# First attention of a two-layer transformer kernel: each step reordered into four stages of two key tiles

## The chip, the cores and the metric

One core of one Trainium2 chip. The metric is the device time of one execution in microseconds (us); the whole two-layer program is one launch. Everything is fp32 at the interface. Four engines compute: TensorE (PE, with its weight loads shown as PEld), VectorE (DVE), ScalarE (ACT) and GpSimd (POOL); SyncE (SP) issues the DMAs.

## The reference

Two pre-layernorm layers over x of shape (2, 1024, 128). Only the first attention matters here:

```python
q = z @ wq @ fcq_w + fcq_b
k = z @ wk @ fck_w + fck_b
v = z @ wv @ fcv_w + fcv_b          # 16 heads of 64
scores = jnp.einsum('bihd,bjhd->bhij', q, k) / scale
attn = jax.nn.softmax(scores, axis=-1)
out = jnp.einsum('bhij,bjhd->bihd', attn, v)
return out.reshape(b, n, N_HEAD * D_V) @ fco_w + fco_b
```

After it come a mixture of experts, a second (causal) attention with rotary parts, and a second mixture of experts. None of their code changes.

## The kernel before

The first attention (`l0_attention`) runs 16 steps, two batches of 8 head pairs. Step n does the attention of its own pair, and beside it prepares step n + 1 and finishes step n - 1. The engines follow one script per step, `step_script(n)` (L391), which TensorE, ScalarE and VectorE all walk; two tables, `AFTER_SCORES` and `AFTER_VALUES` (L375 to L383), say where the small units stand in it. Its items:

- **ST(kt, j)**, the scores of key tile kt (of 8, 128 keys each) for query half j, transposed (keys on partitions), both heads: 4 matmuls of 128x512 in fp32r (L931, L932), accumulating two operand parts. The array is used whole (128x128). ScalarE takes the exponential into `prob[kt % 4]` (L680).
- **PV(kt, j)**, the values: fp32 matmuls of 64 columns by 512, the two heads side by side in the two column halves of the array (L904), accumulating over kt in `pv`. One PV is 4 matmul records (two heads, each fp32 product in two passes).
- **s(x)**, x = 0 to 15, for the next step: the scores of 128 queries against 512 keys, only to find each query's maximum; the two heads use the two row halves of the array, 64 rows each (L863, L865), and VectorE reduces the tile (L738, `mx`).
- **q(j)**: the next step's projection, 4 fp32r matmuls on the whole array (L854), rounded and copied by ScalarE (L638), the rest taken by VectorE (L732).
- **m**: VectorE takes the larger of the two key halves' maxima (`mmax`, L742), TensorE turns them (L883, 16 rows), VectorE makes a row of them (`mrow`, L747), and a DMA (L528) writes it as row 0 of `q2`, where the next step's score matmuls (L932) read it as the shift of the softmax. Before its first ST, step n waits for that row (`row_loaded`, L925).
- **l, r, n, g** for the step before: softmax sums through a matmul with ones (L888, 32 columns of the array), reciprocal, normalisation (L775), output projection in fp32 on the whole array (L893) and the addition into the output (L779). **R, X, P** are early pieces of the next layer that stand in three of the last steps.

Each ST and each unit that TensorE writes takes the next of three PSUM tiles `pair0` to `pair2` (`RING = 3`), in the order of the script; before it writes one, TensorE waits until the tile three places earlier has been read (`await_buffer`, L479). GpSimd adds the `prob` tiles up for the sums (L623, L628). In steps 0 to 11 a piece of the later layers' weights is loaded, split in two parts (ScalarE L655, VectorE L812, after the step's units) and stored.

Before the change a step is, for each key tile: two ST, then the units of `AFTER_SCORES`, then the two PV of the key tile before, then those of `AFTER_VALUES`. The PV of the last key tile stand in the next step. Runs of matmuls that use the array in one way are thus: ST ST | s s | PV PV | s | and so on.

## Time and profile before

| | us |
|---|---|
| median of 3 runs (1487.17 to 1487.96) | 1487.65 |
| the profiled execution's own time | 1486.37 |
| its span, first to last instruction | 1484.6 |
| first attention, from the first score of step 0 to the end of the last matmul for the sums | 63.84 to 747.85 |
| mean granted TensorE clock over the span | 0.972 |

How to read the profile: busy is the time in which at least one instruction of the engine runs. Matmul records overlap (one of 512 columns lasts 0.39 to 0.50 us but the next begins 0.23 us later), so TensorE's progress is read from the start of one matmul to the start of the next, not from durations. A timeline row gives start, length, engine, line, operation, tiles and count, and in brackets how long the engine sat idle before it and what ended that.

### The profile page before, as it was taken

The page shows a single profiled execution, that of the slowest core. Times are in us where ns is not written, and L with a number is a line of the kernel's source. Part 1 is how long each engine was busy: PE and PEld are TensorE (multiplying, and loading weights), DVE is VectorE, ACT ScalarE, POOL GpSimd, SP SyncE. Part 2 cuts the span into 40 slices and gives each one's busy share as a digit, 9 for nine tenths or more (in the row PEclk, how much of TensorE's full clock was granted, in tenths as well). Part 3 has the DMA queues.
Part 4 walks back from the last instruction along what each step waited for, and adds up shares of the span by engine and source line. Part 5 has one row for each costly group of instructions (what it writes and reads, how often), then busy time and mean ns, then how long its engine had stood idle before and what let it go on. Part 6 is the DMA issues. An engine that isn't in the chain of part 4 may idle for free. (4 is left out here: it accounts for less than half of the span.)

```text
span 1484.6 us, 18636 instructions
## 1 busy us (share of the span) xinstructions
PE 1381.6 (93%) x6322; PEld 783.4 (53%) x6322; DVE 999.2 (67%) x1675; ACT 817.5 (55%) x1236; POOL 863.1 (58%) x685
## 2 busy tenths in 40 slices
PE   6699999999999999999978977899999997999998
PEld 5344444444444444544456734454444445787776
DVE  5676777777677777677666678676666725566665
ACT  4244444444444445444545443566776565787776
POOL 0298777777977777787744505455565332344443
PEclk9699999999999999999999997999999998999999
DMA  3110111111011111000050005012111106000000
GB/s 107 33 44 16 58 59 44 58 58 48 26 58 58 51 52 44 15 16 15 26 159 1 1 0 100 15 24 30 21 30 29 30 2 271 1 1 8 8 8 8
DMA packets 32586, 60.59 MB, mean 41 GB/s; under 512 B 9499, under 2 KB 17084, under 8 KB 32348
## 3 DMA queue, kind: packets, MB, share of 16 engines
q1 hardware_dynamic: 32492, 59.40, 14.4%
q8 instruction: 51, 0.84, 0.2%
q14 instruction: 43, 0.35, 0.1%
HBM read 35.13 MB, written 13.89 MB: 33 GB/s over the span
## 5 line engine op out<-in xcount | busy, mean ns | idle before, releaser
L628 POOL TENSOR_TENSOR psum_k<-psum_k,prob 128x1024 f32<-128x1024 f32 x186 | 457.9, 2485 | 46.5 <-ACT prob L680 46.5
L680 ACT ACTIVATE prob<-pair 128x1024 f32<-128x1024 f32 x256 | 250.5, 1025 | 378.7 <-PE pair L932 378.7
L738 DVE TENSOR_REDUCE mx<-pair 128x2 f32<-128x1024 f32 x256 | 305.3, 1222 | 100.0 <-PE pair L865 99.5
L904 PE MATMUL pv<-prob,c_all 128*64 128x512 f32 x1024 | 247.9, 605 | 0.0
L1935 DVE CUSTOM_DVE_ANT_0 l_banks<-l_banks,causal 128x128 f32<-128x128 f32 (+7 forms) x256 | 189.5, 782 | 75.8 <-PE l_banks L1973 74.7
L931 PE MATMUL pair<-qq,ak 128*128 128x512 f32 x512 | 221.5, 433 | 7.1 <-DVE q L732 3.3
L1843 ACT ACTIVATE l_prob<-l_banks 128x1024 f32<-128x1024 f32 (+7 forms) x256 | 155.3, 654 | 111.7 <-PE l_banks L1992 111.0
L932 PE MATMUL pair<-q,kb 128*128 128x512 f32 x512 | 202.4, 395 | 0.0
L2151 POOL TENSOR_TENSOR silu_rest_t<-silu_t,silu_lead_t 128x512 fp32r<-128x512 f32 x74 | 96.4, 1304 | 145.0 <-ACT silu_lead_t L2348 145.0
L1897 POOL TENSOR_SCALAR_AFFINE_SELECT l_prob<-l_prob 128x128 f32<-128x128 f32 x256 | 72.3, 295 | 146.9 <-ACT l_prob L1843 145.3
L623 POOL TENSOR_TENSOR psum_k<-prob 128x1024 f32<-128x1024 f32 x31 | 74.1, 2412 | 118.9 <-ACT prob L680 118.9
L931 PEld LDWEIGHTS pair<-qq,ak 128*128 128x128 f32 x512 | 96.6, 189 | 73.2 <-issue 22.8
L2517 DVE TENSOR_TENSOR silu_t<-silu_t,bank_t 128x512 f32<-128x512 f32 x128 | 88.0, 688 | 64.4 <-ACT silu_t L2339 60.4
L1973 PE MATMUL l_banks<-l_kk,l_qq 128*128 128x512 f32 (+3 forms) x384 | 115.4, 394 | 14.1 <-DMA l_qq<-rounded 4.7
L2339 ACT ACTIVATE silu_t<-bank_t,b_t 128x512 f32<-128x512 f32 x144 | 99.3, 690 | 41.8 <-PE bank_t L951 41.6
L904 PEld LDWEIGHTS pv<-prob,c_all 128*64 128x64 f32 x1024 | 62.1, 136 | 112.6 <-issue 80.6
L863 PE MATMUL pair<-ak,qq 64*128 64x512 f32 x256 | 112.8, 487 | 9.0 <-DVE mx L738 5.0
L1992 PE MATMUL l_banks<-l_qq,l_kk 128*128 128x512 f32 (+3 forms) x384 | 112.1, 385 | 4.2 <-DVE plain L1935 3.2
L865 PE MATMUL pair<-kb,qq 64*128 64x512 f32 x256 | 113.1, 488 | 0.0
L863 PEld LDWEIGHTS pair<-ak,qq 64*128 64x128 f32 x256 | 47.0, 188 | 122.0 <-issue 94.6
L932 PEld LDWEIGHTS pair<-q,kb 128*128 128x128 f32 x512 | 96.9, 189 | 19.8 <-issue 3.3
L1973 PEld LDWEIGHTS l_banks<-l_kk,l_qq 128*128 128x128 f32 x384 | 64.9, 199 | 73.7 <-ACT l_prob L1843 23.6
(318 smaller groups left out, 2276.8 us busy)
## 6 DMA issues: line engine op xcount, KB each, us to landing
plain<-scratch_sums SPq DMA_DIRECT2D x32, 256.0 KB
whole<-in_experts SPq DMA_DIRECT2D x12, 512.0 KB, 5.1
scratch_lead<-rounded SPq DMA_DIRECT2D x12, 512.0 KB, 2.6
scratch_rest<-rounded SPq DMA_DIRECT2D x12, 512.0 KB, 3.9
w_lead_t<-scratch_lead SPq DMA_DIRECT2D x9, 512.0 KB, 6.6
w_rest_t<-scratch_rest SPq DMA_DIRECT2D x9, 512.0 KB, 7.4
l_kk<-rounded SPq DMA_DIRECT2D x16, 256.0 KB, 4.2
l_qq<-rounded SPq DMA_DIRECT2D x16, 256.0 KB, 5.4
```

Source lines behind the costliest of these rows:

```text
L628: nc.gpsimd.tensor_tensor(total[:, h, :], total[:, h, :], prob[kt % 4][:, h, :], ALU.add).then_inc(summed, 1)
L680: nc.scalar.activation(prob[kt % 4][:, :, ts(j, BLK)], buffer("ST", at)[:, :, :], ACT.Exp, scale=D0 ** -0.5).then_inc(exp_done, 1)
L738: nc.vector.reduce_max(mx[:, x % 2, :, x // 2], buf[:, :, :], AX.X).then_inc(read, 1)
L863: nc.tensor.matmul(buf[:, 0, :], qq[k % 2][0][0:D0, ts(t, P)], m.ak[0:D0, keys], start=True, stop=True)
L865: ins = nc.tensor.matmul(buf[:, 1, :], qq[k % 2][1][D0:P, ts(t, P)], m.kb[D0:P, keys], start=True, stop=True)
L904: ins = nc.tensor.matmul(pv[D0 * h:D0 * (h + 1), ts(j, BLK)], m.c_all[:, TT * (s // PAIRS) + kt, :], prob[kt % 4][:, h, ts(j, BLK)], start ...
L931: nc.tensor.matmul(buf, m.ak[:, keys], qq[n % 2][h][:, ts(j, BLK)], start=True, stop=False)
L932: ins = nc.tensor.matmul(buf, m.kb[:, keys], q2[n % 2][:, h, ts(j, BLK)], start=False, stop=True)
L1843: nc.scalar.activation(prob[kt % 2][:, g, P * kt:T], buffer(item)[:, P * kt - T:], ACT.Exp, scale=SCALE1).then_inc(exp_done, 1)
L1935: ins = nc.vector.tensor_tensor_reduce(scores[:, 0:s_width(t)], scores[:, 0:s_width(t)], hidden, 1.0, -3e38, ALU.add, ALU.max, mx[:, g, t: ...
L1973: ins = nc.tensor.matmul(out[:, lo:end], qq[k % 2][:, g, ts(t, P)], kk[k % 2][:, g, lo:end], start=True, stop=True)
L1992: ins = nc.tensor.matmul(buf[:, at:at + end - lo], kk[n % 2][:, g, ts(kt, P)], qq[n % 2][:, g, lo:end], start=True, stop=True)
```

## The change

The two tables give way to one, `STAGES`, that writes a step as four stages of two key tiles. Stage 0 holds four ST together, q(0), four PV (key tiles 6 and 7 of the step before) and l. Stages 1 to 3 hold four ST each, and between them all 16 s units (6, 5 and 5), then four PV of the two key tiles of the stage before. In stage 3 the PV are broken by m and g. The PV of the last two key tiles stand in the next step (of the last step: behind the loop). The larger of the two halves' maxima is no longer taken by VectorE ahead of m: TensorE turns both halves (two matmuls), and VectorE reduces over them in PSUM and then makes `mrow`. On the SP queue the row of shifts (`shift_rows`) now goes ahead of the row of maxima. ScalarE's early work of the next layer hangs on later key tiles.

```diff
--- before.py
+++ after.py
@@ -372,15 +372,17 @@
             + [("l", 0), ("r", 0), ("n", 0), ("g", 0)] * k_done)
 
 
-AFTER_SCORES = {
-    0: [("q", 0), ("q", 1)],
-    1: [("s", 1), ("s", 2)], 2: [("s", 4), ("s", 5)], 3: [("s", 7), ("s", 8)], 4: [("s", 10), ("s", 11)],
-    5: [("s", 13), ("s", 14)],
-}
-AFTER_VALUES = {
-    0: [("s", 0)], 1: [("s", 3), ("l", 0)], 2: [("s", 6), ("X", 0)], 3: [("s", 9), ("r", 0)], 4: [("s", 12)],
-    5: [("s", 15)], 6: [("m", 0), ("n", 0), ("R", 0), ("P", 0)], 7: [("g", 0)],
-}
+STAGES = [
+    ["ST", "ST", "ST", "ST", ("q", 0),
+     "PV", "PV", "PV", "PV", ("l", 0)],
+    [("s", 0), "ST", "ST", ("s", 1), "ST", ("s", 2), "ST", ("s", 3), ("q", 1), ("s", 4), ("s", 5),
+     "PV", "PV", "PV", "PV", ("X", 0), ("r", 0)],
+    [("s", 6), "ST", "ST", ("s", 7), "ST", ("s", 8), "ST", ("s", 9), ("s", 10),
+     "PV", "PV", "PV", "PV", ("n", 0)],
+    [("s", 11), "ST", ("s", 12), "ST", ("s", 13), "ST", ("s", 14), "ST", ("s", 15),
+     "PV", "PV", ("m", 0), "PV", ("g", 0), "PV", ("R", 0), ("P", 0)],
+]
+STRIDE = TT // len(STAGES)
 
 
 STATISTICS_BEHIND = (3, 8)
@@ -392,12 +394,15 @@
 
     has = step_units(n + 1 < STEPS0, n > 0) + EARLY.get(n, [])
     out = []
-    for kt in range(TT):
-        out += [("ST", kt, 0), ("ST", kt, 1)]
-        out += [("UNIT",) + u for u in AFTER_SCORES.get(kt, []) if u in has]
-        if kt or n:
-            out += [("PV", kt - 1, 0), ("PV", kt - 1, 1)]
-        out += [("UNIT",) + u for u in AFTER_VALUES.get(kt, []) if u in has]
+    for stage, items in enumerate(STAGES):
+        at = {"ST": 2 * STRIDE * stage, "PV": 2 * STRIDE * (stage - 1)}
+        for item in items:
+            if item in at:
+                if at[item] >= 0 or n:
+                    out.append((item, at[item] // 2, at[item] % 2))
+                at[item] += 1
+            elif item in has:
+                out.append(("UNIT",) + item)
     return out
 
 
@@ -463,7 +468,6 @@
         on = sb("on", [P, T])
         ones = sb("ones", [P, D0])
         mx = sb("mx", [P, 2, 2, TT])
-        mmax = sb("mmax", [P, 2, TT])
         tcol = sb("tcol", [2 * TT, P])
         mrow = sb("mrow", [2 * TT, P], F32R)
         whole = sb("whole", [P, PIECE])
@@ -487,7 +491,7 @@
         row_loaded, m.sums_moved, inv_ready = sem("row_loaded"), sem("sums_moved"), sem("inv_ready")
         sums_moved = m.sums_moved
         filled, read = sem("work_filled"), sem("work_read")
-        hi_done, mmax_ready = sem("hi_done"), sem("mmax_ready")
+        hi_done, top_ready = sem("hi_done"), sem("top_ready")
         st_filled, exp_done, pv_done, ut_ready = sem("st_filled"), sem("exp_done"), sem("pv_done"), sem("ut_ready")
         summed, norm_done = sem("summed"), sem("norm_done")
         piece_in, piece_led, piece_split, piece_kept = (sem("piece_in"), sem("piece_led"), sem("piece_split"),
@@ -586,8 +590,8 @@
                 if n:
                     sums(n - 1, place(n, ("l", 0)))
                 if n + 1 < STEPS0:
+                    shift_rows(n + 1)
                     max_rows(n + 1, place(n, ("m", 0)))
-                    shift_rows(n + 1)
             sums(LAST, first_of(STEPS0))
             sp.wait_ge(row_loaded, 32 * STEPS0)
             sp.wait_ge(cols_loaded, 16 * STEPS0)
@@ -664,7 +668,7 @@
                             project(n + 1, rest[1], place(n, tuple(rest)))
                     elif what == "PV":
                         kt, j = rest
-                        if kt < 0:
+                        if kt == -1:
                             keep_product(n - 1, j)
                     else:
                         kt, j = rest
@@ -681,30 +685,30 @@
                                              scale=D0 ** -0.5).then_inc(exp_done, 1)
                         if j and kt in (4, 5) and piece_of(n) is not None:
                             lead_piece(piece_of(n), kt - 4)
-                        if j and kt == 2 and n == AT_TURN:
+                        if j and kt == 3 and n == AT_TURN:
 
                             act.wait_ge(read, place(PAIRS, ("g", 0)) + 1)
                             act.wait_ge(piece_split, 2 * len(PIECES))
                             nc.scalar.activation(turned[:, :], m.out_t[:, 0:T], ACT.Identity, bias=m.out_bias[:, 0:1]
                                                  ).then_inc(early_act, 1)
-                        if j and kt == 6 and n == AT_ROOT:
+                        if j and kt == 7 and n == AT_ROOT:
                             act.wait_ge(m.aggr_done, NBLK + 2)
                             nc.scalar.activation(m.std0[:, 0:HALF], m.mv[:, 0:HALF, 1], ACT.Sqrt, bias=m.eps[:, 0:1]
                                                  ).then_inc(early_act, 1)
-                        if j and kt < 2 and n == AT_LOGITS:
+                        if j and kt in (1, 3) and n == AT_LOGITS:
 
                             act.wait_ge(early_dve, CENTRE)
                             act.wait_ge(read, place(AT_TURN, ("R", 0)) + 1)
-                            for t in range(TPB * kt, TPB * (kt + 1)):
+                            for t in range(TPB * (kt // 2), TPB * (kt // 2 + 1)):
                                 ins = nc.scalar.activation(normal[:, t, :], m.x[:, t, :], ACT.Identity,
                                                            bias=m.centre[:, t:t + 1], scale=m.rstd0[:, t:t + 1])
                             ins.then_inc(early_act, 1)
-                        if j and kt == 4 and n == AT_LOGITS:
+                        if j and kt == 5 and n == AT_LOGITS:
 
                             act.wait_ge(read, place(AT_LOGITS, ("X", 0)) + 1)
                             act.wait_ge(piece_kept, 32 * len(PIECES))
                             nc.scalar.copy(m.early_x[:, 0, :], xt[:, :]).then_inc(early_act, 1)
-                        if j and kt == 0 and n == LAST:
+                        if j and kt == 1 and n == LAST:
                             act.wait_ge(early_dve, SHIFTED)
                             nc.scalar.activation(m.ex[:, :, :], m.lg[:, :, :], ACT.Exp).then_inc(early_act, 1)
             for j in R2:
@@ -736,15 +740,14 @@
                 elif kind == "s":
                     v.wait_ge(filled, u + 1)
                     nc.vector.reduce_max(mx[:, x % 2, :, x // 2], buf[:, :, :], AX.X).then_inc(read, 1)
-                    if x == S_UNITS - 1:
-
-                        v.wait_ge(read, u + 1)
-                        nc.vector.tensor_tensor(mmax[:, :, :], mx[:, 0, :, :], mx[:, 1, :, :], ALU.max
-                                                ).then_inc(mmax_ready, 1)
                 elif kind == "m":
                     v.wait_ge(cols_loaded, 16 * (k + 1))
                     v.wait_ge(filled, u + 1)
-                    nc.vector.scalar_tensor_tensor(mrow[:, :], buf[0:2 * TT, 0, 0:P], -1.0, tcol[:, :],
+                    top = buf[0:2 * TT, 1, 0:P]
+                    nc.vector.reduce_max(top, buf[0:2 * TT, 0, 0:2 * P].rearrange("p (a n) -> p n a", a=2), AX.X
+                                         ).then_inc(top_ready, 1)
+                    v.wait_ge(top_ready, k + 1)
+                    nc.vector.scalar_tensor_tensor(mrow[:, :], top, -1.0, tcol[:, :],
                                                    ALU.mult, ALU.subtract).then_inc(read, 1)
                 elif kind == "l":
                     v.wait_ge(filled, u + 1)
@@ -879,9 +882,11 @@
                         ins = nc.tensor.matmul(buf[:, 0, ds(NEXP * t, NEXP)], xt[:, ts(t, P)], m.wr[:, :],
                                                start=True, stop=True)
                 elif kind == "m":
-                    pe.wait_ge(mmax_ready, k + 1)
-                    ins = nc.tensor.matmul(buf[0:2 * TT, 0, 0:P], mmax[:, :, :].rearrange("p h t -> p (h t)"),
-                                           m.ident[:, :], start=True, stop=True)
+                    pe.wait_ge(read, place(k - 1, ("s", S_UNITS - 1)) + 1)
+                    for half in R2:
+                        ins = nc.tensor.matmul(buf[0:2 * TT, 0, ts(half, P)],
+                                               mx[:, half, :, :].rearrange("p h t -> p (h t)"), m.ident[:, :],
+                                               start=True, stop=True)
                 elif kind == "l":
                     await_sums(pe, k, TT - 1)
                     for q in range(4):
@@ -932,8 +937,9 @@
                             ins = nc.tensor.matmul(buf, m.kb[:, keys], q2[n % 2][:, h, ts(j, BLK)],
                                                    start=False, stop=True)
                         ins.then_inc(st_filled, 1)
-            for j in R2:
-                product(STEPS0 - 1, TT - 1, j)
+            for kt in range(TT - STRIDE, TT):
+                for j in R2:
+                    product(LAST, kt, j)
             u = first_of(STEPS0)
             unit("l", 0, u, LAST)
```

How the order moves, at three places. Names: `pair0` to `pair2` are the ring of PSUM tiles, qq and ak, kb and q2 the operands of the scores, and the brackets name the semaphores that a row waits for (work_read: a unit's tile was read; exp_done: an exponential was taken).

TensorE, a key tile in the middle of a step, before:

```order
L931 MATMUL pair1<-qq00,ak 128x512 [waits work_read]
L932 MATMUL pair1<-q2_0,kb 128x512
L931 MATMUL pair1<-qq01,ak 128x512
L932 MATMUL pair1<-q2_0,kb 128x512
L863 MATMUL pair2<-ak,qq10 128x512 [waits work_read]
L865 MATMUL pair2<-kb,qq11 128x512
L863 MATMUL pair0<-ak,qq10 128x512 [waits hi_done,exp_done]
L865 MATMUL pair0<-kb,qq11 128x512
L904 MATMUL pv<-prob2,c_all 64x512 [waits exp_done]
L904 MATMUL pv<-prob2,c_all 64x512
L904 MATMUL pv<-prob2,c_all 64x512 [waits exp_done]
L904 MATMUL pv<-prob2,c_all 64x512
```

and with the change, a piece of stage 2:

```order
L866 MATMUL pair1<-ak,qq10 128x512 [waits work_read]
L868 MATMUL pair1<-kb,qq11 128x512
L936 MATMUL pair2<-qq00,ak 128x512 [waits exp_done]
L937 MATMUL pair2<-q2_0,kb 128x512
L936 MATMUL pair2<-qq01,ak 128x512
L937 MATMUL pair2<-q2_0,kb 128x512
L866 MATMUL pair0<-ak,qq10 128x512 [waits hi_done,exp_done]
L868 MATMUL pair0<-kb,qq11 128x512
L936 MATMUL pair1<-qq00,ak 128x512 [waits work_read]
L937 MATMUL pair1<-q2_0,kb 128x512
L936 MATMUL pair1<-qq01,ak 128x512
L937 MATMUL pair1<-q2_0,kb 128x512
```

What moved: two ST in a row (8 matmuls) and two s in a row have become one ST, one s, one ST, one s; the PV went behind the stage.

TensorE, around the maxima at the end of a step, before:

```order
L904 MATMUL pv<-prob1,c_all 64x512 [waits exp_done]
L904 MATMUL pv<-prob1,c_all 64x512
L883 MATMUL pair2<-ident,mmax 16x128 [waits mmax_ready,work_read]
L931 MATMUL pair0<-qq00,ak 128x512 [waits exp_done]
L932 MATMUL pair0<-q2_0,kb 128x512
L931 MATMUL pair0<-qq01,ak 128x512
L932 MATMUL pair0<-q2_0,kb 128x512
L931 MATMUL pair1<-qq00,ak 128x512 [waits exp_done]
```

and with the change:

```order
L909 MATMUL pv<-prob0,c_all 64x512 [waits exp_done]
L909 MATMUL pv<-prob0,c_all 64x512
L887 MATMUL pair1<-ident,mx 16x128 [waits work_read]
L887 MATMUL pair1<-ident,mx 16x128
L909 MATMUL pv<-prob1,c_all 64x512 [waits exp_done]
L909 MATMUL pv<-prob1,c_all 64x512
L898 MATMUL pair2<-on,g_all 128x512 [waits norm_done,exp_done]
L898 MATMUL pair2<-on,g_all 128x512
L909 MATMUL pv<-prob1,c_all 64x512 [waits exp_done]
L909 MATMUL pv<-prob1,c_all 64x512
```

What moved: m has two matmuls and waits for the last reduction itself; the unit g, which stood directly ahead of the next step's scores, is now between two PV.

VectorE, the same place, before:

```order
L738 TENSOR_REDUCE mx<-pair0 128x2 [waits work_filled]
L742 TENSOR_TENSOR mmax<-mx 128x16 [waits work_read]
L747 SCALAR_TENSOR_TENSOR mrow<-pair0,tcol 16x128 [waits work_filled,cols_loaded]
L775 TENSOR_TENSOR on<-plain 128x1024 [waits ut_ready,sums_moved]
L779 TENSOR_TENSOR plain<-pair0,plain 128x1024 [waits work_filled]
L812 TENSOR_TENSOR rounded<-whole,rounded 128x512 [waits piece_kept,piece_led] x2
L732 SCALAR_TENSOR_TENSOR q2_0<-pair0,q_bias,qq00 64x512 [waits hi_done]
```

and with the change:

```order
L742 TENSOR_REDUCE mx<-pair2 128x2 [waits work_filled]
L742 TENSOR_REDUCE mx<-pair1 128x2 [waits work_filled]
L747 TENSOR_REDUCE pair2<-pair2 16x128 [waits work_filled,cols_loaded]
L750 SCALAR_TENSOR_TENSOR mrow<-pair2,tcol 16x128 [waits top_ready]
L782 TENSOR_TENSOR plain<-pair0,plain 128x1024 [waits work_filled]
L815 TENSOR_TENSOR rounded<-whole,rounded 128x512 [waits piece_kept,piece_led] x2
L736 SCALAR_TENSOR_TENSOR q2_0<-pair2,q_bias,qq00 64x512 [waits hi_done]
```

What moved: `mmax` is gone, a reduction from PSUM into PSUM stands ahead of `mrow`, and the normalisation (`on`) has gone up to the end of stage 2.

## Rows read from the trace of the kernel before

**Rows 1.** The page, busy time of each engine, share of the span, instructions.
```profile
PE 1381.6 (93%) x6322; PEld 783.4 (53%) x6322; DVE 999.2 (67%) x1675; ACT 817.5 (55%) x1236; POOL 863.1 (58%) x685
```
**Rows 2.** Stretches, one per step: length; busy PE, PEld, DVE, ACT, POOL; clock; DMA.
```profile
63.84:104.56 40.72, 39.63 (x163) 20.33 (x163) 27.24 (x24) 19.11 (x22) 28.46 (x12) 0.96 0.04 14
104.56:146.51 41.95, 41.95 (x185) 20.74 (x183) 27.44 (x26) 19.88 (x24) 35.30 (x16) 1.00 0.16 52
146.51:189.54 43.03, 42.63 (x184) 20.62 (x183) 31.25 (x28) 19.96 (x24) 33.93 (x15) 1.00 0.16 50
...
620.64:663.27 42.63, 42.32 (x185) 20.64 (x183) 30.06 (x42) 21.69 (x25) 33.12 (x15) 1.00 0.06 14
663.27:710.30 47.03, 45.37 (x209) 23.27 (x207) 35.90 (x33) 23.02 (x31) 35.67 (x15) 1.00 0.07 21
710.30:747.85 37.55, 37.53 (x158) 16.80 (x156) 25.50 (x45) 18.30 (x22) 25.31 (x9) 1.00 0.06 15
```
**Rows 3.** Timeline of step 7, one key tile: PV, s, ST, s.
```profile
377.65 1.94 PE L904 MATMUL pv<-prob,c_all 128*64 128x512 f32 x8
378.13 0.14 PEld L904 LDWEIGHTS pv<-prob,c_all 128*64 128x64 f32 x2 [0.28 <-ACT prob L680]
...
378.56 0.14 PEld L904 LDWEIGHTS pv<-prob,c_all 128*64 128x64 f32 x2 [0.29 <-issue]
...
379.52 0.50 PE L863 MATMUL pair<-ak,qq 64*128 64x512 f32 x1
...
379.95 0.50 PE L931 MATMUL pair<-qq,ak 128*128 128x512 f32 x1
...
380.06 1.23 DVE L738 TENSOR_REDUCE mx<-pair 128x2 f32<-128x1024 f32 x1 [0.21 <-PE pair L865]
380.29 0.40 PE L932 MATMUL pair<-q,kb 128*128 128x512 f32 x1
...
380.52 0.40 PE L931 MATMUL pair<-qq,ak 128*128 128x512 f32 x1
...
382.01 0.50 PE L863 MATMUL pair<-ak,qq 64*128 64x512 f32 x1
```
**Rows 4.** Timeline of step 7, the unit m and what follows.
```profile
399.00 0.39 PE L883 MATMUL pair<-ident,mmax 128*16 128x128 f32 x2
...
399.32 0.50 PE L931 MATMUL pair<-qq,ak 128*128 128x512 f32 x1
```
**Rows 5.** Timeline, turn from step 6 to step 7.
```profile
360.21 1.98 PE L893 MATMUL pair<-on,g_all 128*128 128x512 f32 x4
...
361.63 0.80 PE L931 MATMUL pair<-qq,ak 128*128 128x512 f32 x1
...
362.26 0.40 PE L932 MATMUL pair<-q,kb 128*128 128x512 f32 x1
...
363.37 3.47 DVE L812 TENSOR_TENSOR rounded<-whole,rounded 128x512 fp32r<-128x512 f32 x2
...
366.87 2.77 DVE L732 SCALAR_TENSOR_TENSOR q<-pair,q_bias,qq 64x512 fp32r<-64x512 f32 x4
...
367.66 0.49 PE L863 MATMUL pair<-ak,qq 64*128 64x512 f32 x1
...
368.35 0.50 PE L931 MATMUL pair<-qq,ak 128*128 128x512 f32 x1 [0.20 <-DVE q L732]
...
370.95 0.50 PE L863 MATMUL pair<-ak,qq 64*128 64x512 f32 x1
```
**Rows 6.** ScalarE's exponentials, steps 3 to 12: duration ns min/median/max.
```profile
L680 ACT ACTIVATE prob<-pair x160: 1016/1026/1030, 191.1 to 617.5; 128x1024 f32<-128x1024 f32 x160
```
**Rows 7.** Timeline, ahead of step 0: the row of maxima and the first score.
```profile
61.90 0.60 SPq L528 DMA_DIRECT2D q<-mrow  x1
...
63.84 0.77 PE L931 MATMUL pair<-qq,ak 128*128 128x512 f32 x1 [2.37 <-issue]
```
**Rows 8.** Timeline of step 6, VectorE's maximum of two halves.
```profile
353.44 1.58 DVE L742 TENSOR_TENSOR mmax<-mx 128x16 f32<-128x16 f32 x1
```

## Prediction

> **What bounds the kernel now.** I read the page first: TensorE is busy 93% of the span, the next engine (VectorE) 67% [rows 1]. An average says little, so I cut the first attention into its steps. A typical step lasts 43.03 us, and in it TensorE is busy 42.63, GpSimd 33.9, VectorE 31.3, ScalarE 20.0, at granted clock 1.00 [rows 2]. Step 2 is shown; steps 3 to 11 last as long to 0.02 us, so what is said of one holds for all. Busy time doesn't tell whether TensorE streams or only drains, so the timeline is next, read from start to start.
>
> In one key tile [rows 3] four PV (two items, 8 records) take from 377.65 to 379.52, 1.87 us; one s unit takes 0.43 to the next ST; two ST take from 379.95 to 382.01, 2.06 us. Inside a run the pitch is 0.23 us per fp32r matmul (380.29 to 380.52) and 0.43 per fp32 pair (weight loads at 378.13 and 378.56); the two heads of an s unit run at once and count as one. So the content is 8 x 0.23 = 1.84 for the two ST, 0.23 for s, 4 x 0.43 = 1.72 for the PV, and what is over, 0.20 to 0.22, 0.20 and 0.15, comes once for each run that uses the array in one way. The first gap of a run shows half of it: 379.95 to 380.29 is 0.34, not 0.23. I call it the price of a run: **0.20 us for an fp32r run, 0.15 for a PV run.** Where the shape stays the same nothing is paid: the unit g takes 1.42 to the following ST, and that one's first gap is 0.63 where 0.34 is usual, together 1.71 us = 4 x 0.43 [rows 5].
>
> The rest are waits. Behind the turn of a step, s lasts 0.69 (367.66 to 368.35) and two ST 2.60 (to 370.95) [rows 5]: 0.26 and 0.54 over their usual, **0.80 us**. The cause stands beside: VectorE finishes the rest of the weight piece (from 363.37, 3.47 us) and only then takes q (from 366.87), so the ring tiles of q come free late. Further on in the step the key tiles repeat rows 3, with nothing waiting. TensorE's own sequence is therefore the bound, and the change has to be counted in runs.
>
> **The change, part by part**, for one step.
>
> *Runs.* Before, a step has 8 runs of ST (q and g join one), 11 of s, 8 of PV, and l and m: 29. After: whole-array runs 1 + 4 + 3 + 4 (stage 0 joins four ST and q(0); in stages 1 to 3 each s breaks the ST) and g, which now stands alone between PV: 13. Runs of s: 5 + 4 + 5 = 14. Runs of PV: one in each of stages 0 to 2, three in stage 3 (broken by m and g): 6. With l and m 35. That is 8 fp32r runs more, 8 x 0.20 = +1.60 us, and 2 PV runs fewer, -0.30 us. The price of a run of four ST is not in the trace. Bounds: 0, as where q follows ST in the same shape (a pair of runs that differ in nothing but weights), and 0.22, as for eight ST. It is nearest to the latter, since the neighbours (s on row halves) are the same; I take 0.20.
>
> By the Trainium skill (TensorEngine Tiling (Array Packing), Key Properties) a change of tiling mode drains the array; this speaks against the change, and the trace agrees on when a price is paid. For its size the skill has only a nearby figure (TensorE: Matmul & The Clock Gate, Single matmul latency: 398 cycles besides the columns, 0.166 us warm); the estimate from that page would make the 8 runs 1.33 us, and the sum of all steps 4 us lower, 1496 us.
>
> *m.* Two matmuls take the place of one. m lasted 0.32 us [rows 4]; with twice the records between 0.40 and 0.64, I take 0.56: +0.24 us. VectorE loses `mmax`, 1.58 us [rows 8], and gains a short reduction. mmax lay beside PV and cost nothing where PV follow; it costs nothing now. If it had been exposed, m would have waited: no row shows that.
>
> *The turn of the step.* Four ST, q(0), then 3.6 us of PV and 1.0 of l, before s(0) at 9.4 us. VectorE's piece ends 5.2 us into the step, half of q's 2.77 follows: 1.4 us, done by 7.8 even if ScalarE is late. The wait of 0.80 us goes, and nothing is late in its place. q(1) is covered by the PV of stage 1.
>
> *The ring.* New borders are tight. From the start of an s to that of the ST two places on is 0.43 + (0.34 + 3 x 0.23 + 0.10 = 1.13) + 0.43 = 1.99 us. In that time the tile must be filled (0.54 from s's start at 379.52 to the reduction's at 380.06) and reduced, 1.23 [rows 3]; with 0.05 allowed for the signal that is 1.82. Margin 0.17 us. From an ST to the s two places on: filled after 1.23 (its 1.03 and the same 0.20), exponential 1.03 [rows 6], 0.05, against 1.13 + 0.43 + 1.13 = 2.69: margin 0.38. Two s in a row at a stage's end leave some 0.05. Nobody waits, by 0.05 to 0.4 us. GpSimd's 33.9 us still fit: the last exponential comes some 6 us before the step's end, two tile sums of 4.8 each follow it, and l reads them 8.4 us into the next step.
>
> *The row of maxima.* The DMA must land before the next step's first ST. From its issue to that ST went 1.94 us when nothing covered it (61.90 to 63.84) [rows 7]. From the start of m: 0.56, fill 0.2, VectorE about 0.8, DMA 1.94: 3.5 us. TensorE meanwhile has m 0.56, two PV 1.0, g 1.9, two PV 1.0: 4.5 us. Margin 1.0 us. In step 0 there is no g, and about 1.0 us of wait appears. `shift_rows`, now ahead on the SP queue, costs nothing: it waits only for work of the step before; it takes its 0.6 us of issue out of the way.
>
> *Sum.* +1.60 - 0.30 + 0.24 - 0.80 = **+0.74 us** per step: 43.8 us for 43.03. Eleven steps (2 to 12) make 8.1. Steps 1 and 13 lasted 41.95 and 42.63 [rows 2] with little of the wait to give back: +1.5 each, 3.1. Step 14 lasted 47.03 [rows 2], 43.03 + 2.65 for its two early units + 1.35 of waits, which go for the most part: 0. Step 0 (40.72) has its row wait and s(0) right behind q(0); the last (37.55) has 4 ST runs in place of 8, but the two PV of a key tile more behind the loop: +1.0 together, between -1 and +3. In all **+12.2 us**. The profiled execution took 1486.37, so 1498.6 there; the median is 1.3 us above it: **1500 us**. Nothing after the attention changes; it starts later as a whole. With the price at 0.17 to 0.22, m at its bounds and the ends at theirs this case reaches from 1495 to 1505.
>
> **Rivals.**
>
> *Cheap short runs (faster).* Perhaps a run of four ST between s units costs less than one of eight, for instance because the weights of the next run are already in. Place: the 8 added runs of stages 1 to 3. 120 runs in 15 steps; the sum is zero at 0.20 - 12.2/120 = 0.10 us per run, and at 0.05 the time is 1482, at 0 it is 1476. For it: q behind ST is free. Against it: s runs of one and of two units both pay the same 0.20. Chance 0.10, and 0.05 that it lands near 0.10 and the time within 0.2%, about what a measurement here can tell from no change (1485 to 1491).
>
> *A new wait (slower still).* If reductions, exponentials or semaphores take 0.1 us more than I allow, the borders of ST and s wait, 12 a step: 1.2 x 15 = 18 us, 1518; at half the borders 1509. Or the row of maxima comes late: 1 us over its margin is 15 us, 1515. For it: the margins of 0.05 to 0.4 us, and VectorE has 16 reductions in 34 us instead of 43. Against it: the exponentials last 1.016 to 1.030 us [rows 6], and the steps are alike to 0.02 us. Chance 0.15.
>
> *The change doesn't do what it says*: merged PV runs would save nothing if the pair pitch at their joint were longer; that is 0.15 x 4, at most 9 us, and belongs to the case above.
>
> **How the numbers follow.** Forecast (1495 to 1505): 0.70. New waits: 0.15. Cheap short runs: 0.10. Near no change: 0.05. Slower by over 0.2%: 0.85, within: 0.05, faster: 0.10. The range leaves out the far half of each rival: 1493 to 1510.
>
> **What would show it.** A step of 43.8 us in the stretches; behind an s, ST ST of 1.13 us for one item; q(0)'s wait gone; PV runs of 16 records lasting 3.6 us. Wrong if one ST between two s lasts under 1.03 us from start to start, or if the timeline shows TensorE waiting for `mx`, the exponential, or the row of maxima in every step.

## Result, and the profile after

| | before | changed |
|---|---|---|
| median of 4 runs, us | 1487.41 (1486.70 to 1487.96) | 1511.42 (1509.54 to 1514.05) |
| the profiled execution's own time | 1486.37 | 1514.05 |
| its span | 1484.6 | 1512.3 |
| first score of step 0 | 63.84 | 65.01 |
| end of the first attention | 747.85 | 775.99 |
| a typical step | 43.03 | 44.83 |

The ratio is 1.0163 (1.0145 to 1.0181): the change makes the kernel 24 us slower, where I forecast 12 us slower. The time lies 1.4 us above the end of the range.

The page after, busy time by engine, beside rows 1:

```profile
PE 1399.9 (93%) x6354; PEld 787.3 (52%) x6354; DVE 976.9 (65%) x1675; ACT 824.7 (55%) x1236; POOL 857.7 (57%) x685
```

The stretches, one per step, the first two, step 7 and the last three (columns as in rows 2):

```profile
65.01:107.20 42.19, 39.93 (x156) 20.95 (x157) 24.83 (x24) 19.64 (x22) 30.96 (x14) 0.93 0.05 13
107.20:152.02 44.82, 43.77 (x184) 20.76 (x185) 30.61 (x28) 20.49 (x24) 35.42 (x15) 1.00 0.16 48
376.19:421.02 44.83, 43.78 (x186) 20.76 (x185) 29.54 (x29) 20.49 (x24) 33.76 (x15) 1.00 0.15 49
646.03:690.84 44.81, 43.82 (x187) 20.73 (x186) 30.41 (x43) 22.36 (x25) 33.11 (x14) 1.00 0.05 13
690.84:738.59 47.75, 46.76 (x210) 23.34 (x209) 30.96 (x31) 23.34 (x31) 34.39 (x15) 1.00 0.07 20
738.59:775.99 37.40, 37.40 (x166) 17.98 (x165) 26.30 (x46) 17.94 (x22) 21.55 (x7) 1.00 0.06 16
```

TensorE is busy 18 us longer in all. Steps 3 to 11 are alike again (44.83 each but for 0.01). Against rows 2 the first score comes 1.2 us later, step 0 lasts 1.5 more, step 1 2.9, each of the steps 2 to 12 1.8, step 13 2.2, step 14 0.7, and the last 0.15 less: 28.1 us, where the spans differ by 27.7. What follows the attention lasts 736.8 us before and 736.3 after. So the typical step is what has to be explained: **+1.80 us where +0.74 was forecast**. And TensorE in step 7 is busy 43.78 of 44.83 us: a whole microsecond of a step is idle, where I had left none.

The order's own pace is in the timeline of step 7, stages 0 and 1:

```profile
381.00 3.65 PE L909 MATMUL pv<-prob,c_all 128*64 128x512 f32 x16
...
385.58 0.50 PE L866 MATMUL pair<-ak,qq 64*128 64x512 f32 x1
...
386.01 0.50 PE L936 MATMUL pair<-qq,ak 128*128 128x512 f32 x1
...
388.07 0.50 PE L866 MATMUL pair<-ak,qq 64*128 64x512 f32 x1
...
388.50 0.50 PE L936 MATMUL pair<-qq,ak 128*128 128x512 f32 x1
...
389.62 0.50 PE L866 MATMUL pair<-ak,qq 64*128 64x512 f32 x1
```

Sixteen PV records take 3.58 us to the next start (381.00 is the first; l follows at 384.58, s(0) at 385.58), an s unit 0.43 (385.58 to 386.01), and one item's ST between two s 1.12 (388.50 to 389.62). That is 4 x 0.23 + 0.20: a short run pays the full price. The lengths that the forecast gave for a PV run, an ST, l and m came out within 0.05 us.

The idle time stands at one place of the step, the turn from stage 2 to stage 3. The timeline of step 6:

```profile
355.88 10.34 POOL L632 TENSOR_TENSOR psum_k<-psum_k,prob 128x1024 f32<-128x1024 f32 x4 [2.04 <-ACT prob L684]
...
358.34 2.36 DVE L742 TENSOR_REDUCE mx<-pair 128x2 f32<-128x1024 f32 x2 [0.35 <-PE pair L868]
...
360.61 3.37 DVE L778 TENSOR_TENSOR on<-plain 128x1024 f32<-128x1024 f32 x1
...
362.06 0.50 PE L866 MATMUL pair<-ak,qq 64*128 64x512 f32 x1
...
362.50 0.50 PE L936 MATMUL pair<-qq,ak 128*128 128x512 f32 x1
...
363.63 0.50 PE L866 MATMUL pair<-ak,qq 64*128 64x512 f32 x1
...
363.91 2.34 DVE L742 TENSOR_REDUCE mx<-pair 128x2 f32<-128x1024 f32 x2
...
365.18 0.49 PE L936 MATMUL pair<-qq,ak 128*128 128x512 f32 x1 [1.05 <-DVE mx L742]
```

The ST at 365.18 would have begun at 364.06, one s after 363.63. It waits 1.12 us for a ring tile: that of s(11), written at 362.06, which VectorE begins to reduce only at 363.91. What holds VectorE is the normalisation `on` (L778): 3.37 us, from 360.61 to 363.98. It stood at the end of the step before the change and stands at the end of stage 2 now. Its durations (minimum, median, maximum ns), before and after, one row of each kernel's trace:

```profile
L775 DVE TENSOR_TENSOR on<-plain x13: 2079/2086/2089, 141.6 to 658.3; 128x1024 f32<-128x1024 f32 x13
```

```profile
L778 DVE TENSOR_TENSOR on<-plain x13: 2571/3374/3374, 136.4 to 676.1; 128x1024 f32<-128x1024 f32 x13
```

2.09 us there, 3.37 here, nearly always the same. While it runs, GpSimd adds `prob` tiles (from 355.88, four adds in 10.34 us). With 2.09 us `on` would have ended at 362.70, just as s(11) was filled; its reduction would have been done by 363.93, and nobody would have waited. The same wait is 1.12 us in each of the steps 1 to 12, 1.06 in step 13 and 0.89 in step 14, 15.4 us in all.

The single adds around `on` show where its time goes. In step 6 before, with `on` beside the add that was under way when it began and the next one:

```profile
355.32 2.38 POOL L628 TENSOR_TENSOR psum_k<-psum_k,prob 128x1024 f32<-128x1024 f32 x1 [0.33 <-ACT prob L680]
...
356.69 2.09 DVE L775 TENSOR_TENSOR on<-plain 128x1024 f32<-128x1024 f32 x1
...
357.65 3.34 POOL L628 TENSOR_TENSOR psum_k<-psum_k,prob 128x1024 f32<-128x1024 f32 x1
```

and in step 6 after, where `on` began at 360.61:

```profile
360.54 2.37 POOL L632 TENSOR_TENSOR psum_k<-psum_k,prob 128x1024 f32<-128x1024 f32 x1
...
362.85 3.37 POOL L632 TENSOR_TENSOR psum_k<-psum_k,prob 128x1024 f32<-128x1024 f32 x1
```

Both times `on` ends 1.07 to 1.08 us behind the end of the add under way (357.70 and 362.91). Before, 1.01 us of that add was left when `on` began; after, 2.30.

### The profile page after: what moved, and what is told of

The parts are those of the page before. It is cut to its first block and busy times, and to the rows that moved or that the text cites. A ratio compares the mean times of both kernels' runs of the same rounds, so it can differ in the third digit from the quotient of the medians.

```text
span 1512.3 us, 18700 instructions
## 1 busy us (share of the span) xinstructions
PE 1399.9 (93%) x6354; PEld 787.3 (52%) x6354; DVE 976.9 (65%) x1675; ACT 824.7 (55%) x1236; POOL 857.7 (57%) x685
## 5 line engine op out<-in xcount | busy, mean ns | idle before, releaser
L684 ACT ACTIVATE prob<-pair 128x1024 f32<-128x1024 f32 x256 | 253.6, 1025 | 364.5 <-PE pair L937 364.3
L909 PE MATMUL pv<-prob,c_all 128*64 128x512 f32 x1024 | 240.2, 601 | 0.0
L866 PE MATMUL pair<-ak,qq 64*128 64x512 f32 x256 | 124.2, 504 | 8.1 <-DVE mx L742 5.0
L909 PEld LDWEIGHTS pv<-prob,c_all 128*64 128x64 f32 x1024 | 65.2, 136 | 125.2 <-issue 114.6
L868 PE MATMUL pair<-kb,qq 64*128 64x512 f32 x256 | 124.1, 503 | 0.0
```

The costliest lines, as they stand in the source:

```text
L684: nc.scalar.activation(prob[kt % 4][:, :, ts(j, BLK)], buffer("ST", at)[:, :, :], ACT.Exp, scale=D0 ** -0.5).then_inc(exp_done, 1)
L866: nc.tensor.matmul(buf[:, 0, :], qq[k % 2][0][0:D0, ts(t, P)], m.ak[0:D0, keys], start=True, stop=True)
L868: ins = nc.tensor.matmul(buf[:, 1, :], qq[k % 2][1][D0:P, ts(t, P)], m.kb[D0:P, keys], start=True, stop=True)
L909: ins = nc.tensor.matmul(pv[D0 * h:D0 * (h + 1), ts(j, BLK)], m.c_all[:, TT * (s // PAIRS) + kt, :], prob[kt % 4][:, h, ts(j, BLK)], start ...
```

## Experiments

Two theories stood. **Contention:** `on` is 1.28 us longer since it collides with GpSimd's adds, and that alone makes the idle time; the rest is the runs, as forecast. **Order:** the wait is the ring's own (margins of 0.05 to 0.4 us), or the runs cost more than counted, and `on` is only what the trace happens to name. The first four experiments are compared with one set of runs of the kernel before (median 1487.80), the other four with another (1487.94).

**1 and 2. GpSimd's sums made short, in the changed kernel and in the one before.**

```diff
- nc.gpsimd.tensor_tensor(total[:, h, :], total[:, h, :], prob[kt % 4][:, h, :],
+ nc.gpsimd.tensor_tensor(total[:, h, 0:8], total[:, h, 0:8], prob[kt % 4][:, h, 0:8],
...
```

The first sum of a step is cut in the same way, so these two kernels leave out the sums of the other columns, and their results are not those of the kernel before. The two tiles of sums are filled with ones once, at the start.

> The changed kernel, with GpSimd's sums of the exponentials cut from 1024 to 8 columns each (the sums of the other columns are left out; instructions, semaphores and waits stay). In the changed kernel a step lasts 44.83 us, 43.71 of it TensorE's own sequence and 1.12 a wait for the maximum s(11), which VectorE takes late because its normalisation lasted 3.37 us. Theory A (that operation from SBUF into SBUF is held up by GpSimd's adds): it lasts about 1.2 us here, the wait is gone, a step lasts 43.7, and the time falls by 15 x 1.12 = 17 us, to about 1494. Theory B (it waits for its DMA or is slow by itself): the step stays at 44.8 and the time within 3 us of 1511.

> The kernel before, with the same sums cut to 8 columns. If a step is TensorE's runs plus the 0.80 us behind VectorE's part of the weight piece, which GpSimd's adds draw out, that part falls from 3.47 to about 1.4 us and the wait goes: 42.2 us for steps 2 to 11 and 1478 to 1479 in all. Together with the run before it this leaves the two orders without any wait: 43.7 against 42.2, 1.5 us a step, as counted from 35 runs against 29. If the added runs were not what costs, the two would come within 0.5 us a step.

Measured: the changed kernel 1498.88 us (1496.38 to 1499.89), ratio to the kernel before 1.0073 (1.0053 to 1.0093), steps of 43.70. The kernel before 1475.89 (1475.08 to 1476.32), ratio 0.9925 (0.9907 to 0.9942), steps of 42.19. The row of one step of the first, and its `on`:

```profile
368.65:412.35 43.70, 43.70 (x187) 20.77 (x185) 27.30 (x29) 20.49 (x24) 2.51 (x14) 1.00 0.16 50
```

```profile
L780 DVE TENSOR_TENSOR on<-plain x13: 1215/1216/1217, 135.7 to 661.7; 128x1024 f32<-128x1024 f32 x13
```

and one step of the second:

```profile
357.82:400.01 42.19, 42.19 (x184) 20.78 (x183) 26.78 (x28) 19.83 (x24) 2.51 (x14) 1.00 0.16 52
```

TensorE is busy in every part of both steps, and `on` takes 1.216 us. No wait is left at the turn to stage 3 with the ring unchanged, so the ring's own margins held: this speaks for contention. The difference of the two orders without waits is 43.70 - 42.19 = 1.51 us; the forecast's count of runs and of m was 1.60 - 0.30 + 0.24 = 1.54. The first kernel missed its expectation of 1494 by 5 us, and the attention is not where they are: it ends at 759.66 in place of 775.99, 16.3 us earlier: 15.4 of waits, and 0.8 by which it begins earlier. What follows the attention, whose code is the same, took 738.4 us in place of 736.3, and the expectation had started from the median, 2.6 us under the profiled execution (both below, under the level of the time). The second kernel came 2 us under its expectation of 1478 to 1479.

**3. The changed kernel, with the normalisation on GpSimd** between its own adds, where it can't collide with them.

```diff
+                    if kt == 5 and n:
+                        pool.wait_ge(sums_moved, 64 * n)
+                        pool.wait_ge(ut_ready, 2 * n)
+                        if n >= 2:
+                            pool.wait_ge(filled, place(n - 1, ("g", 0)) + 1)
+                        nc.gpsimd.tensor_tensor(on[:, :], ut[:, :], rb[:, :], ALU.mult).then_inc(norm_done, 1)
...
-                    nc.vector.tensor_tensor(on[:, :], ut[:, :], rb[:, :], ALU.mult).then_inc(norm_done, 1)
```

Besides, the DMA that refills `rb` now waits for the normalisation before (`norm_done`).

> The changed kernel, with the normalisation done by GpSimd between its sums of key tiles 4 and 5 instead of by VectorE at the end of stage 2. Theory A: s(11) is read in time, a step lasts 43.7 us, 1494 to 1497 in all; GpSimd has 34 + 2.4 us of work in it. Theory B gives the same here if VectorE's operation is slow by itself, and no gain if the DMA of the inverse sums is late, since GpSimd would then hold up its own sums.

Measured: 1499.98 us (1498.30 to 1502.98), ratio 1.0088 (1.0065 to 1.0110). One step, and GpSimd's timeline ahead of it:

```profile
367.65:411.34 43.69, 43.69 (x186) 20.76 (x184) 27.64 (x28) 20.49 (x24) 35.12 (x16) 1.00 0.16 50
```

```profile
348.46 4.70 POOL L640 TENSOR_TENSOR psum_k<-psum_k,prob 128x1024 f32<-128x1024 f32 x2 [2.04 <-ACT prob L692]
353.12 2.41 POOL L627 TENSOR_TENSOR on<-plain 128x1024 f32<-128x1024 f32 x1
355.48 7.06 POOL L640 TENSOR_TENSOR psum_k<-psum_k,prob 128x1024 f32<-128x1024 f32 x3
```

The sums are all there, the wait is gone, and a step takes 43.69 us, as in experiment 1. The normalisation takes 2.41 us, longer than VectorE's 1.22, at a place where nobody waits for it. The time is 3 us over the expectation of 1494 to 1497. Again the attention is shorter as it should be (it ends at 759.09, 16.9 us earlier, and begins 1.6 earlier), and what follows it took 739.1 us.

**4. The kernel before, with the rest of the weight piece ahead of g** in steps 1 to 11, to take away the 0.80 us at the turn.

```diff
+                    if kind == "g" and ahead is not None and piece_of(ahead - 1) is not None:
+                        rest_of_piece(piece_of(ahead - 1))
...
-                if piece_of(n) is not None:
+                if n == 0:
                     rest_of_piece(piece_of(n))
```

> The kernel before, with VectorE's part of the weight piece taken ahead of the addition of g (where VectorE sat idle 3.45 us) instead of after it, in steps 1 to 11. If the 0.80 us at the turn of a step come from that part alone, steps 2 to 12 lose them: 42.2 us, 1478 to 1480 in all, faster than both kernels. If q's ring tiles come late for another reason (ScalarE's copies), the step stays at 43.0 and the time at 1487.

Measured: 1498.21 us (1494.13 to 1499.31), ratio 1.0065 (1.0042 to 1.0087): slower, against the expectation. The step grew to 44.03 us:

```profile
366.47:410.50 44.03, 42.55 (x185) 20.71 (x183) 33.33 (x29) 19.95 (x24) 34.83 (x15) 1.00 0.15 49
```

The timeline shows why:

```profile
360.16 11.26 POOL L628 TENSOR_TENSOR psum_k<-psum_k,prob 128x1024 f32<-128x1024 f32 x4 [0.35 <-ACT prob L680]
...
361.53 2.09 DVE L775 TENSOR_TENSOR on<-plain 128x1024 f32<-128x1024 f32 x1
...
363.54 5.64 DVE L814 TENSOR_TENSOR rounded<-whole,rounded 128x512 fp32r<-128x512 f32 x2
...
370.37 2.11 PE L856 MATMUL pair<-aq,w_all 128*128 128x512 f32 x8 [1.48 <-DVE plain L779]
```

The piece's two halves take 5.64 us there, where both took 3.47 at their old place [rows 5] and 1.37 (0.683 each) in experiment 2. GpSimd's four adds take 11.26 us, against some 9.5 for four at its usual pitch. So `g` is added late (by L779), its ring tile comes free late, and q, behind the first scores of the next step, starts 1.65 us late: those scores and the wait last 3.90 us (366.47 to 370.37), where they last 2.25 at the turn of the kernel before. That is twice what the turn gave back. My estimate of the operation's length was off once more by the same cause: what a VectorE operation with two inputs in SBUF lasts depends on where GpSimd's adds are, and I moved it to where they are dense.

**5. The kernel before, with the m part alone**: two turns and a reduction in PSUM in place of `mmax`.

```diff
-                        nc.vector.tensor_tensor(mmax[:, :, :], mx[:, 0, :, :], mx[:, 1, :, :], ALU.max
...
+                    for half in R2:
+                        ins = nc.tensor.matmul(buf[0:2 * TT, 0, ts(half, P)],
+                                               mx[:, half, :, :].rearrange("p h t -> p (h t)"), m.ident[:, :],
+                                               start=True, stop=True)
...
```

> The kernel before with the maxima's part of the change alone: both halves turned by TensorE, the larger taken by VectorE in PSUM, no maximum of 16 columns ahead. By TensorE's runs: m lasts 0.54 us instead of 0.32, 15 x 0.22 = +3.3 us, 1491, if VectorE's weight piece at the turn of the step takes as long as before (3.47 us); between 1482 and 1498 if it moves against GpSimd's adds. Rival (the maximum of halves, 1.58 us, was on the path): faster than 1487.

Measured: 1489.59 us (1486.04 to 1491.43, 10 runs), ratio 1.0007 (0.9997 to 1.0017): no difference that can be measured. m costs its 0.22 us on TensorE, but without `mmax` the operations behind it come at another phase against the adds (`on` 1.41 instead of 2.09, the piece 3.23 instead of 3.47), and the wait at the turn falls from 0.80 to 0.55. The step read here, 42.96 us, is 0.07 shorter; others last up to 43.03. A small term was paid and given back at once; it can't be read from the time.

**6. The kernel before, with ten more runs a step**: in key tiles 1 to 5 ST s ST s in place of ST ST s s. This measures the disputed price by itself.

```diff
+        if kt in (1, 2, 3, 4, 5):
+            out += [("ST", kt, 0)] + pair[:1] + [("ST", kt, 1)] + pair[1:]
...
```

> The kernel before with the suspected cost doubled and nothing else: in key tiles 1 to 5 the two s units, which stood together behind two ST, stand one behind each ST. Same instructions, 10 runs more per step, none fewer. If a run costs 0.20 us whatever its length: 10 x 0.20 = 2.0 us per step, 30 us in all, 1517. Rival (short runs are cheap, what costs in the changed kernel is its one wait): under 1492.

Measured: 1521.92 us (1521.18 to 1523.76), ratio 1.0229 (1.0212 to 1.0246). A step, and TensorE's timeline in one of its key tiles:

```profile
378.17:423.61 45.44, 44.35 (x185) 20.42 (x183) 31.93 (x28) 20.37 (x24) 33.95 (x15) 1.00 0.15 48
```

```profile
397.35 0.49 PE L866 MATMUL pair<-ak,qq 64*128 64x512 f32 x1
...
397.78 0.51 PE L934 MATMUL pair<-qq,ak 128*128 128x512 f32 x1
...
398.91 0.50 PE L866 MATMUL pair<-ak,qq 64*128 64x512 f32 x1
...
399.35 0.50 PE L934 MATMUL pair<-qq,ak 128*128 128x512 f32 x1
...
400.47 0.49 PE L866 MATMUL pair<-ak,qq 64*128 64x512 f32 x1
...
400.90 1.51 PE L907 MATMUL pv<-prob,c_all 128*64 128x512 f32 x6
```

The s take 0.43 (397.35 to 397.78, 398.91 to 399.35, 400.47 to 400.90), the single ST 1.13 and 1.12 us. Two ST together took 2.06 and a second s beside the first 0.23, so each of the ten added runs costs 0.19 to 0.20: 1.9 us of the 2.41 that the step grew by; the wait at the turn, which rose from 0.80 to 1.3, is the other 0.5. The expectation, 1517, counted the runs alone, 2.0 us a step for the 2.41 that came. The rival "cheap short runs" is dead: it asked for 0.10 us a run or less.

**7. The changed kernel, normalisation on GpSimd, and g behind the last values of stage 3**, directly ahead of the next step's scores, as it stood before the change.

```diff
-     "PV", "PV", ("m", 0), "PV", ("g", 0), "PV", ("R", 0), ("P", 0)],
+     "PV", "PV", ("m", 0), "PV", "PV", ("g", 0), ("R", 0), ("P", 0)],
```

> The changed kernel with the normalisation on GpSimd and, besides, g behind the last values of the step instead of between them. g then joins the whole-array run of the next step's scores and one PV run is saved: 0.20 + 0.15 = 0.35 us per step, 43.35 us instead of 43.70, 5 us under the variant with GpSimd alone, about 1495. The row of maxima has 0.6 us of margin left. Rival (place of g doesn't matter): 1500, step 43.70.

Measured: 1493.74 us (1490.51 to 1494.32), ratio 1.0033 (1.0021 to 1.0044); against experiment 3 some 6 us less, and 1 us under the expectation.

```profile
366.11:409.48 43.37, 43.37 (x187) 20.94 (x185) 26.82 (x27) 20.49 (x24) 35.17 (x16) 1.00 0.15 50
```

Steps last 43.34 to 43.37 us, 0.32 to 0.35 less than in experiment 3, for 0.35 counted: one whole-array run fewer at 0.20, one PV run fewer at 0.15. The price per run holds in this direction too. Still it is the slower order: without any wait it takes some 1.16 us more a step than the order before in experiment 2.

**8. The kernel before, with the piece's rest on GpSimd**, behind the sums of key tile 5. The values that are computed are those of the kernel before.

```diff
+                    if kt == 5 and piece_of(n) is not None:
+                        for half in R2:
+                            part = ts(half, PIECE // 2)
+                            pool.wait_ge(piece_led, 2 * n + half + 1)
+                            if n:
+                                pool.wait_ge(piece_kept, 32 * n)
+                            nc.gpsimd.tensor_tensor(w_rest[:, part], whole[:, part], w_lead[:, part].bitcast(F32),
+                                                    ALU.subtract).then_inc(piece_split, 1)
```

> The kernel before, with VectorE's part of the weight piece given to GpSimd (two operations of about 1.2 us behind the sums of key tile 5). VectorE's operations from SBUF into SBUF began only where an add of GpSimd ended; on GpSimd itself the piece waits for nobody. The 0.80 us at the turn go in steps 2 to 12: 42.2 us, 1478 to 1479, faster than both kernels. Rival (GpSimd, then busy 36 of 42 us, is late with the sums for l or for the exponentials): 1485 or more.

Measured: **1479.26 us (1478.02 to 1479.91), ratio 0.9935 (0.9919 to 0.9952)**, faster than both kernels, and as expected to 0.3 us. A step, GpSimd's timeline ahead of it, and the turn of the step:

```profile
358.19:400.38 42.19, 42.19 (x184) 20.80 (x183) 27.70 (x26) 19.84 (x24) 36.40 (x17) 1.00 0.17 51
```

```profile
351.54 2.52 POOL L636 TENSOR_TENSOR rounded<-whole,rounded 128x512 fp32r<-128x512 f32 x2
```

```profile
358.79 1.22 DVE L787 TENSOR_TENSOR plain<-pair,plain 128x1024 f32<-128x1024 f32 x1 [3.66 <-PE pair L899]
...
361.57 2.42 ACT L646 ACTIVATE qq<-pair,q_bias 128x512 fp32r<-128x512 f32 x4
362.29 2.77 DVE L740 SCALAR_TENSOR_TENSOR q<-pair,q_bias,qq 64x512 fp32r<-64x512 f32 x4 [2.28 <-ACT qq L646]
```

GpSimd does both halves in 2.52 us, where VectorE took 3.47 [rows 5]. Behind g's addition VectorE has nothing ahead of q; q's tiles are read at once, and TensorE is busy in all of the 42.19 us, the same step as in experiment 2. The attention ends at 739.39, 8.5 us earlier than before.

## Why the prediction was wrong, and where it was right

*Runs: right.* +1.60 - 0.30 was the main term. The order of the change without waits measures 43.70 us and the order before 42.19; 1.51 for the 1.54 that runs and m made together. The price taken, 0.20, and not the lower bound of 0, was the right choice: 1.12 us for a single ST between s, in the changed kernel and in experiment 6.

*m: right.* 0.54 us for 0.56. VectorE's part, 0.42 and 0.28 us with the signal between, fits:

```profile
372.43 0.42 DVE L747 TENSOR_REDUCE pair<-pair 16x128 f32<-16x256 f32 x1 [1.25 <-PE pair L887]
372.89 0.28 DVE L750 SCALAR_TENSOR_TENSOR mrow<-pair,tcol 16x128 fp32r<-16x128 f32 x1
```

*The turn of the step: right.* The 0.80 us went. That it was the rest of the piece ahead of q is shown by experiment 8, which takes the piece away and regains 0.84.

*The ring: this step failed.* "Nobody waits, by 0.05 to 0.4 us" was worked out from reductions and exponentials alone. It never asked what else stands in VectorE's line there. That `on` has gone up to the end of stage 2, directly ahead of the reduction of s(11), stood in the description of the change, and no term in the sum priced that move: it was put at nothing without a reason. Its duration was not even quoted. At 2.09 us it would have been free; at 3.37 (2.57 and 3.15 in the steps 13 and 14, where it begins later) it costs 15.4 us. The forecast had 43.77 for the step and TensorE's own part is 43.71. The wait is the whole miss.

Experiments 1 and 3 show that the wait hangs on `on` beside the adds: with the adds cut, or with `on` moved to GpSimd, it is gone, and 11 to 13 us with it. That the excess is contention, and no property of the place, is shown by 1: the same operation at the same place takes 1.216 us. And the excess can be worked out to 0.01 us from the add under way (below, in what the runs showed of the hardware).

*The rival "a new wait"* had the time right (1509 to 1518), at 0.15, and the place half right: a border of ST and s. But it had 12 borders a step slipping by 0.1 us; it was one border, by 1.12, and no reduction was longer than allowed.

*The row of maxima: right inside, a little short at the ends.* No step but step 0 waits for it; step 0 waits 0.88 us for the 1.0 forecast. Ahead of the first step m is covered by nothing, and there I counted nothing: the row's DMA is issued at 63.06 in place of 61.90 [rows 7], which are the 1.2 us by which the first score is later. Only 0.7 of them are m's: the last reduction ahead of it already ended at 61.03 in place of 60.52. Step 14 was set at 0 and cost 0.7, most of its 0.9 of waits at the same place.

*The level of the time.* All these count against the profiled execution: it took 1514.05, the slowest of the four. The forecast of 1498.6 there, with 15.4 of waits, gives 1514.0. The median is 2.6 lower, where the forecast had put it 1.3 higher; with that offset it would have been 1515. So it is in part luck that the miss is as small as 1.4 us. The spread goes with the granted clock of TensorE: the changed kernel's four runs took 1514.05, 1511.67, 1511.17 and 1509.54 us at mean granted clocks of 0.970, 0.971, 0.972 and 0.973. It is no property of the change, for the 16 later runs of the kernel before spread over 4.4 us, from 1485.95 (0.969) to 1490.32 (0.966). The stretch behind the attention shows it as well. One row each, after and experiment 3:

```profile
775.99:1512.30 736.31, 664.34 (x3248) 427.87 (x3248) 467.63 (x1108) 475.02 (x811) 319.83 (x454) 0.96 0.16 38
```

```profile
759.09:1498.20 739.11, 670.78 (x3248) 432.21 (x3248) 467.13 (x1108) 474.67 (x811) 319.62 (x454) 0.95 0.16 37
```

The same code takes 2.8 us longer, and it is TensorE that is busy longer (670.8 us for 664.3), at the lower clock. So differences of 2 or 3 us between medians of four runs say little here; the length of the attention says more. Why the clock differs from run to run wasn't tried.

## What to carry to other kernels

Where TensorE is the bound, count an order in runs of one array shape: nothing else in a reordering was as exact, 0.20 us each here for fp32r and 0.15 for the fp32 values. Then walk the other engines' lines once more at each tight border, and for every operation that moved write its duration down as a term of the sum, from a row with the same neighbours: a VectorE operation with two inputs in SBUF has no duration of its own while GpSimd adds in SBUF; here it was what was left of the add under way plus the operation's own work. If VectorE is what a tight ring waits for, give such operations to the engine that they collide with (1479.26 us for 1487.94).

## What the runs showed of the hardware

VectorE's operations with two inputs in SBUF last as long as GpSimd's adds let them. `on` took 1.22 us alone, 1.41 in experiment 5, 2.09 before and 3.37 in the changed kernel; a half of the piece 0.68 alone and 2.8 in experiment 4; the 16 columns of `mmax` 0.18 alone and 1.58 beside the adds [rows 8]. What decides is how much of the GpSimd operation under way is left when VectorE's begins. For `on`, 0.33 us were left in experiment 5, 0.80 in experiment 8 (1.88 us long), 1.01 before, 1.49 in step 13 of the changed kernel (2.57), 2.30 in its steps 1 to 12, and 2.34 in the last step of the kernel before (3.42). Each time its length is what was left plus 1.08 us, to 0.01. A half of the piece takes what is left plus 0.55, and `mmax` what is left plus 0.03. The longest excess over the length alone was 2.2 us in any run; one add takes 2.35 (4.70 for two in experiment 3). GpSimd pays too: the add that begins while `on` waits or works takes 3.34 or 3.37 us, and four adds took 10.34 and 11.26 us in place of 9.5. Reductions and additions that read a PSUM tile weren't touched: 1.23 us for a reduction of a score tile [rows 3], and 1.22 for g's addition, in all kernels.

The Trainium skill has this rule (SBUF — State Buffer, SBUF: two separate sides): a VectorE operation with two SBUF inputs and a GpSimd operation that reads SBUF take one pair of ports as an exclusive lock, and whoever comes second waits for the whole of the other. These rows agree: the wait lasts to the end of the add under way, at most one add, and not over it. I hadn't used the rule in the forecast. By it, as an estimate from the figures above, `on` in a stretch where GpSimd adds without a pause lasts between 1.2 and some 3.5 us, and the 2.09 of its old place could not be carried over.

The other finding: a run of the array in one shape costs the same 0.20 us whether it holds one s unit, four matmuls or eight.
